# Attention stage of a fused attention and mixture-of-experts block: the row maxima turned behind step 6's second-pass scores instead of at the end of step 5, and VectorE's residual of step 4 behind that step's maximum

## The reference

```
x: (8, 512, 512)   ctx: (8, 1601, 128)   16 heads of 32
xn  = layernorm(x)
q   = xn @ Wq.T ;  k, v = split(ctx @ Wkv.T)
s   = (q_h . k_h) / sqrt(32), causal (key <= query), so only 512 context rows count
x   = x + softmax(s) @ v_h, heads joined, @ Wout.T
hn  = layernorm(x)
logits = hn @ router_w.T + router_b      -> (tokens, 512 outputs, 8 experts)
w   = the two largest of softmax(logits) per output, normalised to sum 1, summed over outputs per expert
x   = x + sum_e w[token, e] * (hn @ expert_w[e].T + expert_b[e])
```

## Time and profile before

| | us |
|---|---|
| median of 3 runs | 1936.11 |
| lowest to highest | 1935.78 to 1937.7 |
| profiled execution, its own time | 1936.01 |
| span of its instructions | 1934.3 |
| PE busy | 1898.8 (98%) |
| DVE busy | 1422.3 (74%) |
| ACT busy | 1040.6 (54%) |
| POOL busy | 851.4 (44%) |
| attention stage, about | 41 to 592 |

### The profile page before, as it was taken

One profiled execution on the slowest core, in us unless ns is written; L12 is line 12 of the kernel. 1 busy time (PEld: TensorE's weight loads), 2 busy tenths in 40 slices (PEclk: granted clock), 3 DMA queues, 4 the chain that ended last, 5 costly groups with the idle time before them and its releaser, 6 DMA issues.

```text
span 1934.3 us, 30336 instructions
## 1 busy us (share of the span) xinstructions
PE 1898.8 (98%) x9746; PEld 1507.3 (78%) x9746; DVE 1422.3 (74%) x2823; ACT 1040.6 (54%) x2067; POOL 851.4 (44%) x1021
## 2 busy tenths in 40 slices
PE   7999999999999999999999999999999999999999
PEld 6667767767766888888888888888888888888887
DVE  5777777767768568878788888577777777777752
ACT  4566567567554457877687877633333444333330
POOL 6787778777673145536354445011112221111110
PEclk8999999999999999999999999999999999999999
DMA  6555554554467578787656455722222322222210
GB/s 186 126 136 137 137 142 126 147 146 125 119 182 267 181 239 278 241 250 258 226 193 230 159 216 203 281 98 87 81 81 93 111 101 81 82 98 87 82 43 33
DMA packets 104622, 294.56 MB, mean 152 GB/s; under 512 B 13937, under 2 KB 15985, under 8 KB 99410
## 3 DMA queue, kind: packets, MB, share of 16 engines
q1 hardware_dynamic: 92130, 209.05, 34.0%
q10 hardware_dynamic: 9072, 67.77, 10.6%
q0 software_dynamic: 3328, 16.78, 3.8%
HBM read 150.31 MB, written 109.16 MB: 134 GB/s over the span
## 4 chain that ended last, share of the span: by engine, by line
PE 89%; DVE 4%; DMA 3%; ACT 2%; issue 2%; SPq 1%; ACTq 0%; DVEq 0%
PE pair L283 22%; PE pair L285 22%; PE pair L284 22%; PE pair L777 4%; PE ps L794 4%; PE pair L738 4%; PE ps L283 3%; PE ps L284 3%; PE ps L285 3%; DMA xb<-x 1%; PE ps L814 1%; DVE nmax L1535 1%; ACT pT L1234 1%; DVE pair L1541 1%; PE ps L1014 1%
## 5 line engine op out<-in xcount | busy, mean ns | idle before, releaser
L283 PE MATMUL pair<-w_h,hT 128*128 128x512 f32 x1912 | 747.5, 391 | 1.0 <-ACT ev_b L1380 0.6
L285 PE MATMUL pair<-w_h,hT 128*128 128x512 f32 x1912 | 744.3, 389 | 0.0
L284 PE MATMUL pair<-w_l,hT 128*128 128x512 f32 x1912 | 744.1, 389 | 0.0
L2077 POOL TENSOR_TENSOR logits<-logits,second 128x512 f32<-128x512 f32 x224 | 298.5, 1368 | 593.4 <-DVE second L1758 593.1
L283 PEld LDWEIGHTS pair<-w_h,hT 128*128 128x128 f32 x1912 | 358.9, 188 | 76.8 <-ACT ev_b L1380 1.7
L285 PEld LDWEIGHTS pair<-w_h,hT 128*128 128x128 f32 x1912 | 358.9, 188 | 75.1
L284 PEld LDWEIGHTS pair<-w_l,hT 128*128 128x128 f32 x1912 | 359.0, 188 | 73.5
L1863 DVE SCALAR_TENSOR_TENSOR xb<-pair,c_all,xb 128x512 f32<-128x512 f32 x256 | 191.8, 749 | 179.1 <-PE pair L285 174.3
L1234 ACT ACTIVATE pT<-pair,zero 128x1024 f32<-128x1024 f32 (+3 forms) x256 | 202.5, 791 | 190.0 <-PE pair L777 180.8
L1541 DVE CUSTOM_DVE_ANT_0 pair<-pair,future 128x384 f32<-128x384 f32 (+1 forms) x330 | 179.9, 557 | 116.1 <-PE pair L738 112.3
L1339 ACT ACTIVATE w<-tree 128x512 f32<-128x512 f32 x32 | 20.2, 633 | 389.1 <-DVE tree L1760 389.1
(11 more groups left out here) (206 smaller groups left out, 2632.6 us busy)
## 6 DMA issues: line engine op xcount, KB each, us to landing
logits<-lg_all ACTq DMA_DIRECT2D x32, 1792.0 KB, 8.8
qk_st<-qk SPq DMA_DIRECT2D x367, 128.0 KB, 2.5
lg_all<-ev_a SPq DMA_DIRECT2D x30, 768.0 KB, 8.7
lg_all<-ev_b SPq DMA_DIRECT2D x29, 768.0 KB, 3.5
xb<-x SPq DMA_DIRECT2D x64, 256.0 KB, 4.3
hT_all<-hT SPq DMA_DIRECT2D x32, 512.0 KB, 4.4
hT<-hT_all SPq DMA_DIRECT2D x32, 512.0 KB, 4.0
w_fix<-in_expertT POOLq DMA_DIRECT2D x8, 1024.0 KB, 6.0
```

Of the source, the lines that this page charges most:

```text
L283: pe.matmul(dst, lh, rh, start=start, stop=False)
L284: pe.matmul(dst, lh, rl, start=False, stop=False)
L285: return pe.matmul(dst, ll, rh, start=False, stop=stop)
L2077: pool.tensor_tensor(logits[t % 2][:, e - 1, :], logits[t % 2][:, e - 1, :], second[:], ALU.subtract)\
```

## The change

Three edits, all of order:

1. `TURN` is 6 instead of 5, and on PE the turn is written between step 6's `shifted_scores` and the first-pass scores of head 1, where before it stood at the end of step 5, ahead of `shifted_scores`.
2. On ACT the copy of the turned maxima (`hi_shift`) goes from the end of the first part of step 5 to the head of step 6. On DVE `lo_shift` stays where it was (the condition is rewritten, its step is 6 in both).
3. On DVE a residual that falls on step 4 (`SCALED` is 4) is written behind that step's `maxima` instead of ahead of it.

```
-        TURN = 5
+        TURN = 6
@@ TensorE
                         shifted_scores(n, c, v, final)
+                        if v == TURN and (more or c < KC - 1):
+                            turn_maxima(n + 1, c + 1)
                         g, vv = target(c, v - 1)
...
-                        if v == TURN and (more or c < KC - 1):
-                            turn_maxima(n + 1, c + 1)
@@ ScalarE
+                        if v == TURN and (more or c < KC - 1):
+                            hi_shift(n + 1)
                         src = (s_ps if v % 2 else e_ps) if last and c == KC - 1 else second_pass_of(v)
...
-                        if v == TURN and (more or c < KC - 1):
-                            hi_shift(n + 1)
                         split = SPLIT_LAST if last else SPLIT
@@ VectorE
-                        if v == TURN + 1 and (more or c < KC - 1):
+                        if v == TURN and (more or c < KC - 1):
                             lo_shift(n + 1)
...
-                        i = None if first else summed_block(c, v, last)
-                        if i is not None:
-                            residual(b - 1, i, out_bank(i, last))
+                        done = None if first else summed_block(c, v, last)
+                        if done is not None and v != SCALED:
+                            residual(b - 1, done, out_bank(done, last))
...
                             maxima(n + g, (c + g) % KC, vv, masked(c, v, last))
+                        if done is not None and v == SCALED:
+                            residual(b - 1, done, out_bank(done, last))
```

## The result

| | before | after |
|---|---|---|
| median of the runs compared (16 and 16) | 1935.37 us | 1939.25 us |
| lowest to highest | 1933.39 to 1940.94 | 1937.43 to 1941.6 |
| span of the profiled execution | 1934.3 | 1937.9 |

The ratio is 1.0021, with an interval of 1.0014 to 1.0027: the change costs about 4.0 us. Forecast were 4.1 us, on a median of 1936.11.

A forecast was written before the change was run, and what follows sets the result against it. The prediction took PE as busy 98% of the span, with DVE's list ending last in step 6 of groups 1 and 3. Its terms, +4.3 - 0.2 + 0 = +4.1 us, gave 1940.2 us, range 1933.0 to 1942.5.

The forecast's parts named there:

- The residual's 0.36 us, twelve times: DVE, groups 1 and 3 of batches 1 to 6: work behind the residual 0.35 to 0.36 us later, +4.3 us in all.
- The earlier turn is worth nothing there: PE, same twelve groups: L738 behind the turn leaves 0.49 us earlier, lost at L283 or the next L738; value zero.
- The sum: Whole kernel: +4.3 - 0.2 + 0 = +4.1 us on the profiled 1936.01, median 1940.2 us.
- Group 3: PE: L283 near +1.65, 0.15 earlier; the following L738 from +2.51 to +2.86, 0.35 us later.
- The swap in groups 0 and 2, -0.2 in all: PE: swap worth zero in groups 0 and 2, bound 0.4 us; the -0.2 was for six places in batches 0 and 7.
- SP: Group 1: second row's issue 0.69 us later, with enough margin before its first product; cost nothing, bound +2.0 us.
- More: Rival, end of group 1: SP's rows come late, up to 2.0 us on top, 1942.2 us; chance 0.10.
- A gain: Rival, steps 5 and 6 of twelve groups: the turn's wait mattered, L283 at +1.31; -6.7 us, 1929.3 us; chance 0.10.
- Half taken back: Rival: ACT's exponential doesn't shift with PE, so one delay per batch vanishes; +2.1 us, 1938.0 us; chance 0.15.
- The rule on the drain: DVE: by the Trainium skill full durations add up, delay 0.27 us, sum +3.0, 1939.1 us; the prediction went by the rows instead.

The follow-up runs named there:

- e2: Before with only the residual of step 4 moved behind the maximum, the turn left at the end of step 5; ratio 1.0016.
- e5: After with group 3's residual put back ahead of the maximum, so that it is behind only in group 1; ratio 1.0014.
- e3: After with an extra unread 192-column DVE reduction ahead of step 4's maximum in groups 1 and 3 of batches 1 to 6; ratio 1.0021.
- e4: Before with the extra unread DVE reduction of e3 at the same place, there ahead of the residual; ratio 1.0018.
- e1: Before with only the turn and its copy moved later, the residual left ahead of the maximum; ratio 1.0006.
- e8: e7 with the turn on PE back at the end of step 5; 1931.84 us, ratio 0.9983.
- e7: After with DVE's residual behind the queries' low part in group 1, low part two steps later in group 3, SP's rows ahead of its load; 1931.63 us.
- e6: Before with the residual of step 4 cut to 32 of 512 columns in groups 1 and 3 of batches 1 to 6; ratio 0.9994.

## Why the prediction was right

**The residual's 0.36 us, twelve times: right.** The places stand as worked out: maximum +0.44, residual +0.78, low part +1.38, in eleven of the twelve groups (in batch 3 group 3 all are 0.35 later, by the pause of the last section). e2 shows the whole loss with this edit alone, e5 half of it with half the places, and e3 and e4 show that it is the idle place on DVE. The term was +4.3. In the trace the six groups 1 are 2.26 us longer and the six groups 3 2.34, of which 0.35 are that pause: 4.25 without it. Single groups grew by 0.34 to 0.39 (the pause left out), but for batch 1 group 3 with 0.20, where the low part was already held up in before (+1.16, by ACT's high part).

**The earlier turn is worth nothing there: right.** 4.9 us of waits went from the list, and 4.2 + 2.2 us came at L283 and L738, the two instructions that the prediction names. e1 and e8 against e7 both show the move alone at about zero.

**The sum: closer than its terms.** The stretch has +4.16. It is the 4.25 above and the pause of 0.35, which the prediction didn't have, less 0.34 in the groups 2 and 0.10 in the groups 0, where it had -0.2 in all. That 4.0 were measured and 4.1 forecast is in part luck: the pause makes up for what was missed in groups 0 and 2.

**Group 3.** L283 came at +1.52, where I had +1.65: I had set it 0.20 behind the residual's end, and it starts 0.06 behind it (246.72 + 0.68 against 247.46). Nothing hung on it. The next L738 was forecast at +2.86 and came at +2.78, while the shifted scores behind it are the full 0.36 late. So the loss was right, and by which instruction it enters is 0.08 off.

**The swap in groups 0 and 2, -0.2 in all: too small there.** I had zero for groups 0 and 2, with 0.03 either way. In group 2 L283 comes at +1.85 in place of +1.92, and a group is 0.07 shorter in five of six batches, 0.34 us in all. Why the new order is 0.07 shorter with the same instructions, no run shows. In group 0 the turn comes at +1.96 in place of +1.74, and a group is shorter by nothing to 0.02; the 0.05 that it lost in batch 1 is in e2 too, without the swap. In batch 7, where I left 0 to -1.5 us open, the turn of group 2 has L283 0.25 us earlier, and it is handed back: the rows were issued at +2.90 in both kernels, and L777 waited for them to land. In group 0 the gain ends at the L738 behind the turn's, which leaves at +3.44 in both.

```profile
586.99 0.50 PE L777 MATMUL pair<-qk_st 98*128 98x512 f32 x1 [0.29 <-DMA qk_st<-nm_l]
```

**SP: right.** In five of the six groups 1 the second row's issue went from about +3.88 to about +4.57, by the 0.69 that was worked out (0.75 in batch 5). Batch 2, from which rows 8 are taken, is the exception: there the store took 2.62 us to land in before, so the issue was at +4.44, and with 2.04 us it is at +4.57 in after. L777 of group 2's head moved with L283 (+7.04 to +7.41 in batch 2) and did not wait for the rows in any of batches 1 to 6. So the rival "More" has no trace of itself there.

**The other rivals.** "A gain" is refuted by L283: it didn't follow the turn at +1.31, but DVE's low part at +2.30. e7 shows what this rival had right: with the low part earlier L283 does come earlier. But it comes at +1.72 and not at +1.31, since it still waits for the low part (0.22 us in the line above), and in group 3 POOL's sum leaves 0.13 us, so 2.3 us are to be had and not 6.7. "Half taken back" is refuted by e5 and by the segments: the wait on the exponentials is 4.4 us before and 4.3 after.

**The rule on the drain.** The residual starts 0.34 behind a maximum of 0.43 and L1520 0.60 behind a residual of 0.68, as in the earlier trace rows. By the sentence of the Trainium skill that the prediction draws on (VectorE: DVE Perf Modes, The DRAIN you can't avoid) the delay would have been 0.27 in each place; the groups grew by 0.34 to 0.39. The same section goes on that an instruction that is not held starts earlier, and the starts here agree with that. The ratio's interval, +2.7 to +5.2 us, takes in both sums, so it is the trace that decides here.

## What to carry over

A wait that the profile lists on the busiest engine is worth what is left when everything behind it has been asked the same question: here the next two matmuls depended on the same VectorE list, so the 4.9 us of waits that went from the list gave nothing. On an engine that works through a list, look for what fills the idle place ahead of an instruction whose input isn't ready; moving that filler behind it delays all the rest by the filled part (0.36 us here). If an instruction is to leave the path, it must go behind the last one that somebody waits for, as in e7, not only behind the first.

## What the runs showed beside

**A pause on DVE whose cause is open.** In after, e2, e3, e7 and e8 DVE once starts L1535 0.35 us late, and the profile shows nothing that it waits for. In after it is in batch 3 group 3, and L743 is at 317.44:

```profile
318.23 0.43 DVE L1535 TENSOR_REDUCE nmax<-pair 128x2 f32<-128x256 f32 x1 [0.62 <-PE pair L743]
```

That is +0.79 in place of +0.44. In e2, e7 and e8 it is at the same place, in e3, whose list on DVE is longer, in batch 2 group 1 (an idle stretch of 0.36 put down to "issue"). In before nothing of it shows at that place, where DVE hadn't been waiting; nor does it in e6, where it had. It looks as if it belonged to a place in DVE's instruction list and were hidden as long as work is queued. The count bears out the place: among the trace's records of DVE, its sequencer's included, the late maximum is number 703 (from 0) in after, e2, e7 and e8, and number 447 in e3, exactly 256 before. In before, e1, e5 and e6 number 703 is the residual of batch 3 group 3, which waits for nothing. But number 959, 256 further on, is a maximum that waited 0.7 us in e3 and e4, and it isn't late. So the place is shown and the cause is not. The pause costs after 0.35 us of its 4.0.

**How far the attention stage's neighbours vary.** L743 of the first group starts at 51.9 to 55.8 us in these kernels, from e1 and e2 to e4, with the same instructions ahead of it in all three. That is as much as the whole change is worth. The granted clock of PE goes with it. Between 32 and 56 us it was at half of full speed (1.2 instead of 2.4 GHz) for 6.8 us in e1, 10.2 in e2, e3, e5 and e7, whose first group starts at 51.9 to 52.8, and for 13.7 us in before and e6, 17.1 in after and 20.5 in e4 and e8, where it starts at 54.4 to 55.8.

The same happens once more behind the stretch. In group 0 of batch 7 the L738 at +3.44 has waited 1.4 us in all ten kernels. In e1, e5, e6 and e8 the clock is at half speed for 3.4 us soon after, and this group takes 17.9 to 18.1 us; in the other six it stays full, and the group takes 16.7. The same 3.41 us, from +4.89, in e1 and in before (window, its length, then the busy us and the instructions of PE, PEld, DVE, ACT and POOL, PE's clock, DMA share, GB/s):

```profile
545.38:548.79 3.41, 3.41 (x26) 1.53 (x19) 0.49 (x2) 0.00 (x0) 2.24 (x3) 0.50 0.40 91
```

```profile
548.53:551.94 3.41, 3.41 (x32) 1.89 (x24) 1.74 (x6) 0.83 (x1) 2.25 (x3) 1.00 0.40 90
```

With one trace of each kernel it isn't shown whether this goes with the kernel or with the single execution, so up to 1.4 us of e1's, e5's, e6's and e8's profiled time may be no part of their edits. A stretch that ended at group 1 of batch 7 would have taken it in: for e1 it would read +1.23 us instead of -0.22.

One profiled execution's span says nothing about a change of this size (e3's is 1934.2, that of before 1934.3, though its median is 0.2% above); a stretch inside it does, if the clock was the same in both.
